# A two-convolution ODE block: convolutions in 64x64 array pieces with column parities apart, and fp16 high parts written by ScalarE

## What is computed

```python
def odefunc(t, y):
    h = relu(group_norm(y, gn1_w, gn1_b))
    h = concat_conv(t, h, conv1_w, conv1_b)     # 3x3, pad 1, 33 -> 32 channels, first one is t
    h = relu(group_norm(h, gn2_w, gn2_b))
    h = concat_conv(t, h, conv2_w, conv2_b)
    return group_norm(h, gn3_w, gn3_b)

y1 = scan(lambda y, t: y + odefunc(t, y) / 6, x, ts)    # 6 steps
```

## Time and profile before

| | |
|---|---|
| three runs | 3934.33, 3935.17, 3935.84 us, median 3935.17 |
| profiled execution, span from first to last instruction | 3928.6 us |
| its own time | the table of runs has none apart; median less span is 6.6 us, which lie around the span |
| TensorE matmul / weight load busy | 3592.0 us (91%) / 2039.1 us (52%) |
| VectorE busy | 3342.3 us (85%) |
| ScalarE busy | 2079.6 us (53%) |
| GpSimd busy | 929.9 us (24%) |
| mean granted TensorE clock | 0.970 of full |

### The profile page before, as it was taken

One profiled execution on the slowest core, in us unless ns is written; L12 is line 12 of the kernel. 1 busy time (PEld: TensorE's weight loads), 2 busy tenths in 40 slices (PEclk: granted clock), 3 DMA queues, 4 the chain that ended last, 5 costly groups with the idle time before them and its releaser, 6 DMA issues.

```text
span 3928.6 us, 70526 instructions
## 1 busy us (share of the span) xinstructions
PE 3592.0 (91%) x21844; PEld 2039.1 (52%) x21844; DVE 3342.3 (85%) x7423; ACT 2079.6 (53%) x3169; POOL 929.9 (24%) x1589
## 2 busy tenths in 40 slices
PE   3699999999999999999999999999999999999995
PEld 3455554555555555555555555555555555554553
DVE  7688888888888888888888888888888888888885
ACT  0455565555655556555565545655555555655553
POOL 4022212222122221222212231123211322111211
PEclk7899999999999999999999999999999999999998
DMA  3300033113032130311312113311133112231013
GB/s 79 74 17 16 22 45 84 41 60 70 11 84 62 61 58 10 94 63 41 58 42 83 41 41 58 76 49 41 41 58 84 41 41 62 37 83 49 25 41 99
DMA packets 366284, 210.26 MB, mean 54 GB/s; under 512 B 351104, under 2 KB 351472, under 8 KB 364016
## 3 DMA queue, kind: packets, MB, share of 16 engines
q1 hardware_dynamic: 366064, 207.66, 21.2%
HBM read 104.88 MB, written 77.07 MB: 46 GB/s over the span
## 4 chain that ended last, share of the span: by engine, by line
issue 39%; PE 34%; DVE 14%; POOL 10%; ACT 2%; POOLq 1%; DMA 1%; DVEq 0%; SPq 0%; ACTq 0%
PE cps L1246 30%; POOL xn L516 3%; POOL small L479 3%; DVE hb L973 2%; POOL m L513 2%; POOL xn L521 2%; PE xps L1320 2%; DVE hb L976 2%; ACT z L620 2%; DVE bnt L889 1%; POOL hb L496 1%; DVE bnt L896 1%; DVE small L951 1%; DVE bn L1000 1%; DVE ha L976 1%
## 5 line engine op out<-in xcount | busy, mean ns | idle before, releaser
L1246 PE MATMUL cps<-ha,w 128*128 128x399 f16 (+1 forms) x9216 | 1737.6, 342 | 69.7 <-DVE ha L976 64.5
L1246 PE MATMUL cps<-hb,w 128*128 128x448 f16 x8064 | 1645.0, 360 | 0.0
L608 ACT ACTIVATE z<-cps,bias_now 128x448 f32<-128x448 f32 (+2 forms) x1440 | 875.8, 610 | 1128.3 <-PE cps L1246 1100.9
L1246 PEld LDWEIGHTS cps<-ha,w 128*128 128x128 f16 x9216 | 861.0, 99 | 693.6 <-ACT z L608 61.1
L1246 PEld LDWEIGHTS cps<-hb,w 128*128 128x128 f16 x8064 | 748.9, 100 | 678.8 <-issue 41.5
L479 POOL TENSOR_TENSOR small<-small,half 128x1 f32<-128x1 f32 x304 | 190.3, 626 | 2135.6 <-DVE small L942 2133.8
L496 POOL MEMSET hb<- 64x28 f16 (+2 forms) x1152 | 320.5, 278 | 784.6 <-DVE hb L976 666.2
L889 DVE BATCH_NORM_STATS2 bnt<-z 128x6 f32<-128x448 f32 x672 | 413.1, 621 | 94.7 <-ACT z L608 94.7
L620 ACT ACTIVATE z<-z,small 128x798 f32<-128x798 f32 (+1 forms) x384 | 405.8, 1057 | 120.5 <-DVE small L951 120.5
L982 DVE SCALAR_TENSOR_TENSOR y<-z,small,y 128x784 f32<-128x784 f32 x384 | 457.4, 1245 | 6.7
L896 DVE BATCH_NORM_STATS2 bnt<-z 128x6 f32<-128x385 f32 (+1 forms) x768 | 411.4, 546 | 56.9 <-ACT z L608 50.4
(11 more groups left out here) (135 smaller groups left out, 2352.4 us busy)
## 6 DMA issues: line engine op xcount, KB each, us to landing
xa<-x_dram SPq DMA_DIRECT2D x64, 392.0 KB, 7.9
y<-xa SPq DMA_DIRECT2D x16, 1568.0 KB, 7.7
y_dram<-y SPq DMA_DIRECT2D x64, 392.0 KB, 7.1
xs<-in_x_dram SPq DMA_DIRECT2D x31, 784.0 KB, 8.7
x_dram<-x1s SPq DMA_DIRECT2D x30, 784.0 KB, 5.3
fin<-y_dram SPq DMA_DIRECT2D x30, 784.0 KB, 7.8
fin<-x_dram SPq DMA_DIRECT2D x28, 784.0 KB, 8.3
out_dram<-fin SPq DMA_DIRECT2D x28, 784.0 KB, 3.3
```

The lines of the kernel that those rows point to most:

```text
L608: nc.scalar.activation(z[slot][:, r0 * width:(r0 + r) * width], cps[i % BANKS][:, 0:r * width], ACT.Identity, bias=bias_now[:, conv:conv + ...
L1246: return pe.matmul(ps, w[:, tap, wl, :], h[:, hl, r0 + a:r0 + a + r, b:b + width], start=(n == 0), stop=(n == len(products) - 1))
```

## The change

- **Pieces.** A partition half (64 partitions) now holds one column parity with both row parities. A product from one column parity to another needs two column taps, from a parity to itself one. So a tile needs for each shift of rows and each of the three high/low products 1 or 2 matmuls of 64x64 instead of parts of four 128x128 ones. Two tiles of 7 rows run at a time, p from rows 0 to 27 and q from rows 28 to 55, in two PSUM banks. The rows 28 to 55 are kept with the column parities swapped between the halves. In the stage "X" (12 rounds) the pieces between different parities run, in "Y" (6 rounds) those within one; a round has four matmuls, one in each quarter of the array. There are 4 pairs in a convolution, in the order X0 X1 Y0 X2 Y1 X3 Y2 Y3, and three places for a pair in PSUM. Convolution 1 gives 56 columns and 57 rows (one pair has a tile of 8 rows).
- **fp16 high parts.** `activate` now issues two ScalarE instructions for a part, one that writes the fp16 high part to `ha` or `hb`, one that writes fp32 to `z`. `split` is the subtraction alone.
- **Half images.** Normalisation is 16 ScalarE instructions (`normalise_half`) in place of two GpSimd ones. One PSUM bank (`dps`) serves both DCT matmuls, so each of the eight groups waits for the one before it to be read. `last_add` is VectorE's.
- **Rims and seams.** Rows are copied on GpSimd (`wrap_rows`, `seam`) in place of zeroing; rim matmuls are 20 in a convolution.
- **Order.** The queues of all engines are written anew, and statistics matmuls stand at other places.

```diff
-TILES1 = [8] + [7] * 7
-TILES2 = [8] * 7
+R = 7
+PHASES = (("X", 0), ("X", 1), ("Y", 0), ("X", 2), ("Y", 1), ("X", 3), ("Y", 2), ("Y", 3))
+PAIR_BANKS = ((0, 1, 2, 0), (1, 2, 0, 1), (2, 0, 1, 2), (2, 0, 1, 2))
+PAIR_LAG = ((3, 3, 3, 3), (3, 3, 3, 3), (3, 3, 3, 3), (1, 4, 4, 3))
...
             def activate(slot, kind, k):
...
-                nc.scalar.activation(z[slot][:, lo:lo + n], src[:, lo:lo + n], ACT.Relu,
-                                     bias=col(small, slot, kind, BI), scale=col(small, slot, kind, SC)
-                                     ).then_inc(r_done, 1)
+                hi = (hb_rows if kind == Z1 else ha_rows)(slot, 0, k)
+                nc.scalar.activation(hi, part_rows(src, k), ACT.Relu, **coefs).then_inc(hi_done, 1)
+                nc.scalar.activation(part(z[slot], k), part(src, k), ACT.Relu, **coefs).then_inc(r_done, 1)
...
+            def normalise_half(n):
+                act.wait_ge(s_nb, n - HALVES + 1)
+                for c in range(CQ):
+                    last = nc.scalar.activation(xn[:, c, :], xs[:, c, :], ACT.Identity,
+                                                bias=m0[:, 6, CQ + c:CQ + c + 1], scale=m0[:, 4, c:c + 1])
...
-                if 0 in halves:
-                    dve.wait_ge(r_done, n + k + 1)
-                    nc.vector.tensor_copy(v[:, 0], src).then_inc(hi_done, 1)
-                if 1 in halves:
-                    dve.wait_ge(hi_done, n + k + 1)
-                    nc.vector.tensor_tensor(v[:, 1], src, v[:, 0], ALU.subtract).then_inc(lo_done, 1)
+                dve.wait_ge(r_done, NP * c + k + 1)
+                dve.wait_ge(hi_done, NP * c + k + 1)
+                nc.vector.tensor_tensor(lo, src, hi, ALU.subtract).then_inc(lo_done, 1)
...
+                    return pe.matmul(dst, w[hin * 64:(hin + 1) * 64, kx, a, wl, :], src[:, :, 0:NA],
+                                     start=(what == "X" and n == 0), stop=(what == "Y" and n == len(kinds) - 1))
...
+                rounds = 12 if what == "X" else 6
+                for n in range(rounds):
+                    if n in between:
+                        between[n]()
...
+                    if what == "X":
+                        p_piece(1, 0, n)
+                        p_piece(0, 1, n)
+                        q_piece(0, 0, n)
+                        last = q_piece(1, 1, n)
...
+                        pe.wait_ge(lo_done, NP * c + min(k + 2, NP))
...
-                between = among((2, 0, (Z1, 1)) if kind == FIVE else (1, 9, (Z1, 1)))
+                between = {(1, 6): lambda: statistics_of(Z1, 1)}
...
-                between = among((1, 3, (Z2, 1)) if kind == MID else (2, 0, (Z2, 1)))
+                between = {(0, 0): lambda: statistics_of(Z2, 1)}
```

More of the change, by code:

```diff
@@ L563, in step @@
                 first = posts_before(g, s, kind)
-                for n, (what, slot) in enumerate(POSTS[kind]):
-                    rsqrt(slot, what, first + n)
-                    if what == Z1:
-                        zero_rim(slot, lo + NP * slot, rim + NP * slot, own + PZ * slot)
-                    if kind == MID and (what, slot) == (Z2, 0):
-                        half_rsqrt(HALVES * (g + 1) + s, m0)
-                        centre_half()
-                    if kind == MID and (what, slot) == (Y, 0):
-                        scale_half(HALVES * (g + 1) + s)
@@ L573, in step, with rsqrt_of @@
-                if kind == MID:
-                    with pool.If(g > 0):
-                        last_add(g * HALVES + s)
+                def rsqrt_of(what, slot):
+                    n = first + POSTS[kind].index((what, slot))
+                    rsqrt(slot, what, n)
+                    return n + 1
+                fixes = 2 * (STEPS * g + s)
+                pows = rsqrt_of(Z1, 0)
+                wrap_rows(0, conv_at(g, s, 1), fixes, pows)
+                if kind == FIVE:
+                    rsqrt_of(IZ, 1)
@@ L581, in _ @@
                 step(g, 5, FIVE)
[L582 removed]
+            with pool.Fori(0, STEPS - 1) as s:
                 step(GROUPS - 1, s, LAST_MID)
[L584 to L585 removed]
             step(GROUPS - 1, 5, LAST)
@@ new lines, in step @@
+                split_for(2, 0)
+                split_for(2, 1)
+                stats_of(1, 1)
+                if kind == MID:
+                    half_post(hn, stats_before(g, s, kind) + STATS[MID].index((X0, 0)))
+                split_for(2, 2)
+                if kind == FIVE:
+                    post_of(IY, 0)
+                if kind == FOUR:
+                    start_stats(0, g + 1, (0, 1))
+                split_for(2, 3)
+                if kind == MID:
+                    with dve.If(g > 0):
+                        last_add(g * HALVES + s)
@@ L1267, in needs, with pair_tiles @@
-            def needs(conv, k):
-                rows = (TILES1, TILES2)[conv]
-                parts = (PARTS_A, PARTS_B)[conv]
-                last = offsets(rows)[k] + rows[k] + (0 if conv == 0 else 1)
-                last = min(last, sum(parts))
-                return next(p + 1 for p in range(NP) if offsets(parts)[p] + parts[p] >= last)
-            def tile(slot, conv, k, i, n, t, ready, base, between=()):
-                if k == 0 or needs(conv, k) > needs(conv, k - 1):
-                    pe.wait_ge(ready, base + needs(conv, k))
-                if not (isinstance(n, int) and n + i < BANKS):
-                    pe.wait_ge(evac_done, n + i - BANKS + 1)
-                conv_tile(slot, conv, k, i, t, between)
+            def pair_tiles(conv, k):
+                if conv == 0:
+                    first = (0, R + 1) if k == 0 else (R * k + 1, R)
+                    return (*first, R * k + 1 + HALF, R, 1)
+                return (R * k, R, R * k + HALF, R, 0)
@@ L1391, in step @@
-                between = among((1, 9 if kind == FIVE else 3, (Z2, 0)))
-                if kind not in (FIVE, LAST):
-                    between.update(among((4, 9, (Y, 0))))
-                elif kind == FIVE:
-                    between.update(among((4, 0, (IY, 1))))
-                for k in range(7):
-                    tile(1, 1, k, i, n, s, rim_zero, rim + NP, between)
-                    i += 1
+                    between[5, 0] = lambda: statistics_of(IY, 0)
+                convolve(0, 1, 1, conv_at(g, s, 1), sets + 1, between)
```

938 lines of the change are left out of this document (540 added, 398 removed).

## The result

| | before | after |
|---|---|---|
| median of the runs | 3935.51 us (4 runs) | 4578.81 us (4 runs, 4576.38 to 4583.74) |
| ratio, 95% interval | | 1.1636, 1.1619 to 1.1652 |
| span of the profiled execution | 3928.6 us | 4574.6 us |

What follows compares the result with a forecast made beforehand. It took TensorE as the old kernel's bound and a chain of waits across engines as the new one's: 28 x (86.3 + 6.2) + 20 x (78.9 + 6.2) + 168.9, plus 6.6, gives 4468 us; range 3980 to 4900.

Steps and rivals of the forecast that it cites:

- Rival 1: TensorE's waits do not halve the clock, since a round fills all four quarters: 4170 us; chance 0.24.
- rival 3: TensorE stays the bound because ScalarE and VectorE finish early enough that statistics never hold it: 3526 us; chance 0.12.
- rival 2: Weight loads bound TensorE's rounds at 0.226 us: steps of 102.7 and 92.4 with stretches, 4899 us; chance 0.12.
- 4: Rival: pieces run two at a time on TensorE, a round 0.34 us: 5815 us; chance 0.05.
- 5: Rival: the array's quarters run in turn, a round 0.68 us: over 9000 us; chance 0.03.
- The round of 0.170 us: On TensorE, four 392-column matmuls in four quarters run side by side, costing 0.170 us as columns alone.
- A: Part of a MID step from Z1 of slot 0 to Z1 of slot 1: 20.2 us at full clock.
- B: Part of a MID step from Z1 of slot 1 to Z2 of slot 0: 18.9 us at full clock.
- C: Part of a MID step from Z2 of slot 0 to Z2 of slot 1: 19.2 us at full clock.
- D: Part of a MID step from Z2 of slot 1 back to Z1 of slot 0: 28.0 us at full clock.
- a stretch of 3.4 us at half clock costs 1.7: Behind each of TensorE's four waits in a step; 1.1 in A, 1.7 in the other three, 6.2 us together.
- six rounds of X1: In A after the 1.09 us subtraction; with statistics, the other six rounds and Y0 they take 3.51 us.

Runs made afterwards that it cites:

- run 2: The changed kernel with the fp16 high part written by a VectorE copy in front of each subtraction, ScalarE keeping only its fp32 activation: 4288.93 us, ratio 1.0900.
- (8): The changed kernel with one of the three fp16 products of a convolution left out (rounds 8 and 4, result no longer the convolution): 4265.97 us, ratio 1.0838.
- run 3: The changed kernel with filling matmuls put in front of three statistics waits of TensorE (Z1 slot 1, Z2 slot 0, Z2 slot 1): 4304.82 us, ratio 1.0942.
- (6): The changed kernel with both the fp16 high part back on VectorE and filling matmuls in TensorE's waits, their counts refitted: 4059.75 us, ratio 1.0315.
- Run 1: The changed kernel with TensorE's steps written out one behind the other in place of its step loops: 4556.13 us, ratio 1.1577.
- run 5: The changed kernel with TensorE's steps written out and filling matmuls in front of three of its statistics waits: 4258.92 us, ratio 1.0832.
- run 12: The kernel before the change, with 12 filling matmuls in front of TensorE's wait for squares in each MID step: 3937.82 us, ratio 1.0007.
- runs from 1 to 11: The follow-up kernels built on the changed kernel, each with one or more edits; measured from 3900.21 to 4592.21 us.
- run 9: The changed kernel with VectorE's cast, statistics moved back, filling at the new waits, TensorE's steps written out and an earlier half-image addition: 3900.39 us, ratio 0.9903.

## Why the prediction was right, point by point

**The direction and the mechanism were right.** ScalarE has 60 us of work in a MID step, VectorE 55, and TensorE 73, some 10 of them for its half clock, where TensorE alone had 77.3; and yet the step is longer, because it is a chain of waits. These are busy times of one step. The runs bear it out from three sides: less on ScalarE (2), fewer rounds (8) and faster ones (3) each shorten the step, and the gains of 2 and 3 nearly add (6). Rival 1 (no halving) is excluded by the clock of the rows, rival 3 (TensorE stays the bound) by the waits, and rivals 2, 4 and 5 by the pace of a round.

**The round of 0.170 us** was taken from columns alone, and is 0.170. Four quarters of the array run side by side, the two pieces of p into one PSUM bank. Two pieces at a time would have made it 0.34. The Trainium skill, "TensorEngine Tiling (Array Packing)", section "Gotcha 1: PSUM Pressure", states that different row tiles cannot access one PSUM bank at the same time; the trace does not agree, since here pieces from different row halves write different partitions of one bank at the full pace. The 213 ns that the prediction worked out for four loads of 64 columns from the Trainium skill, "TensorE: Matmul & The Clock Gate", section "LDWEIGHTS (loading the stationary operand)", do not stand either as a bound of the round: 0.17 us hold four loads.

**Terms that held:** the fp16 activation at the price of the fp32 one; no holding of VectorE; ScalarE 60.4 and VectorE 55.4 us; waits of 8.4, 4.7 and 4.4 us at the statistics (9.1, 5.1 and 4.5 forecast) and 2.8 in front of X1 in steps without a branch back (3.2 forecast).

**The terms that were mis-sized.** The sum was 92.5 us for a MID step and 85.1 for the others; measured are 94.5 and 87.4 in the mean of a group (553.0 us against 540.2). From the statistics Z1 of the first step to that of the last, 47 steps make up 93 of the 113 us between the spans (the first group, in which no finished piece is added, is 10 us shorter than the others, and the last group's steps are 85.6 to 88.8). The other 20 lie before and behind, in the 168.9 us that were taken over from the kernel before. To compare the legs, `pre` to `pre` as they were walked, Z1 of slot 0 counts from VectorE's 906.25 in a step of 95.5 us:

| leg | forecast, with its stretch | measured |
|---|---|---|
| A | 21.3 | 23.2 |
| B | 20.6 | 20.3 |
| C | 20.9 | 21.4 |
| D | 29.7 | 30.7 |

There is luck in legs B and C. With the waits filled (run 3) they are 18.1 and 18.8 where the walk has 18.9 and 19.2, so it was 0.8 and 0.4 us too long, and the stretches in them were 0.5 and 0.9 too short.

The first failed step is "a stretch of 3.4 us at half clock costs 1.7". It was the one example that the kernel before had, behind a wait of 2.08 us. Behind waits of 4.4 to 8.4 us the clock stays low for 6.8 and 10.2 us, from before TensorE starts again, and TensorE works 5.0, 5.1 and 4.2 us in them. Half of that is 7.15, and filling them gave 7.1 us where 5.1 were counted (run 3). The second is leg A's "six rounds of X1" right behind the subtraction. X0 itself, which was to be done by then, begins only at 905.36, because of the branch, and runs at half clock; X1 follows it at 909.6 and not at 907.2. Run 1 shows that the branch alone is worth no more than 0.9 us of this, run 5 that branch and clock together are worth 1.8, give or take 0.8.

**The branch was no term of the sum.** Its row shows 0.21 us with 480 matmuls in a step (960 instructions with their loads) and 3.5 with 1312 (2624); the outer loop 3.7 before and 7.3 after. The Trainium skill, "Runtime: NRT & Kernel Launch", section "Instruction fetch mechanics", states that a taken branch whose target is outside the window that the engine holds waits for a fetch. The trace agrees, with one packet of instructions inside each long branch and none inside the short ones. That section of the Trainium skill gives TensorE's instruction memory 2048 instructions; if that is the window, the old step fits and the new one does not. The Trainium skill also calls that window two pages, of 256 instructions each, and by that the old step would not fit, which its 0.21 us contradict. The outer branch doubled because its packet starts later, 4.4 to 5.9 us behind the branch where it was 0.9 to 1.5 before; what fills that time, nothing here explains.

**Where the reading of before was too simple.** "TensorE is the bound" and "the stretch costs 1.7" for the kernel before fell with run 12: its slow stretch costs nothing, since VectorE's next part is late anyway. That the kernel before pays for its own stretch did not enter the sum, but the walk's "76.1 at full clock, TensorE-bound, and 77.8 with its one stretch" charged it. Nor does every wait of 2.08 us bring a stretch: it stands behind 22 of the 28, and the third of the earlier trace rows has none. In rival 2 the stretches add 7.6 us to a MID step and 4.6 to the others, without a reason; 7.6 in both would give 4959 for its 4899.

**What stays open.** Some 45% of the loss are ScalarE's second activations (run 2), and nearly as much the half clock behind the waits (run 3). The other parts of the change, the half image's 16 activations on ScalarE, its one PSUM bank and VectorE's `last_add`, are in all runs from 1 to 11, and what they cost was not tried. Why D fell by 1.5 us in run 9 and not by 3.7 was not tried apart. That the filling acts by the clock alone, and not by something else that a busy array brings, rests on the granted clock of the rows, 0.84 against 0.96 and more, and on the 7.1 us that half of the slow stretches' work would give.

## What to carry to other kernels

Busy time taken off the engine that looks like the bound may be worth nothing where results cross from engine to engine: walk the chain between two statistics before and after, and count what each engine must finish before the next may start. In this kernel the pieces were good and fast; what made them lose was for the greater part a second activation on the path and TensorE standing idle at matmuls placed for another timing. With the cast back on VectorE, the statistics placed anew and the waits filled, the same pieces gave 3900 us, 1% below the kernel before. A matmul that waits belongs behind all work that needs nothing, and filling in front of the wait, never behind it; and filling is worth something only where TensorE's pace is on the chain (runs 3 and 12).

## What the runs showed of the hardware that was not expected

- Longer waits went with longer stretches at half clock: in MID steps 3.4 us behind a wait of 2.1 (kernel before), 6.8 behind 4.4 and 4.7, 10.2 behind 8.4. It is no fixed rule: a wait of 4.7 us that ended at 1293.3 had 3.4 us behind it. With the waits of 4.4 us and more in MID steps the clock fell before TensorE started again (at 928.1 for the 929.4 above), with that of 2.1 some 1.1 to 1.5 us after it. Filling matmuls into columns that nobody reads keep the clock at 1.00 over a whole step (run 9).
- Pieces in different quarters keep their own pace: at half clock the matmuls of 448 columns followed each other at 0.373 us and those of 392 beside them at 0.327, in one convolution stage at the same time (X0 from 876.1, kernel after).
- A backward branch on TensorE took 0.21 us for a short body and 3.3 to 3.9 for a long one, with a packet of 16 KB on the instruction queue inside it; on ScalarE, VectorE and GpSimd it stayed under 0.1 us.
